# Maxima twelve steps ahead of the scores in place of fourteen, in a fused sequence kernel on one core

## The reference, cut to what matters

```
x = x + time_mixing(layernorm(x))
nodes = {-1: layernorm(x)}
for c in range(6):                       # per sequence
    q = ew[c,0] * (nodes[c-1] @ We + be) # k, v the same way, from earlier nodes
    qh, kh, vh = heads of q @ Wq, k @ Wk, v @ Wv      # 8 heads of 16
    attn = softmax(qh @ kh.T / 4)        # 1024 x 1024 for each head
    nodes[c] = act_w[c] * ((attn @ vh) @ Wo) + q
x = x + layernorm(nodes[5])
```

## Time and profile before

| what | us |
|---|---|
| median of three runs | 2273.95 |
| span of the profiled execution | 2273.4 |
| PE busy | 2241.8 (99%) |
| DVE busy | 2053.9 (90%) |
| ACT busy | 1830.3 (81%) |
| POOL busy | 527.6 (23%) |
| fill, from the first maxima matmul to the first score | 58.7 to 105.9 |
| last score, last matmul | 2251.7, 2264.0 |

### The profile page before, as it was taken

How to read it: one execution, slowest core, us unless ns; L and a number is a source line. 1 busy time by engine, 2 the same in 40 slices (tenths; PEclk the granted TensorE clock), 3 DMA queues, 4 the chain that set the end, 5 groups by cost and what they waited for, 6 DMA issues and landing times.

```text
span 2273.4 us, 46471 instructions
## 1 busy us (share of the span) xinstructions
PE 2241.8 (99%) x18091; PEld 855.8 (38%) x18091; DVE 2053.9 (90%) x2255; ACT 1830.3 (81%) x3431; POOL 527.6 (23%) x667
## 2 busy tenths in 40 slices
PE   7999999999999999999999999999999999999997
PEld 3534333333334333333333333333333333333332
DVE  6998999999999999999999998999999999999994
ACT  4267888888888888888888888888888888888885
POOL 4331330221312202202212112112023022321403
PEclk9999999999999999999999999999999999999999
DMA  4130322423313314224223223133133132342201
GB/s 129 59 67 23 81 65 55 84 67 67 79 46 91 71 33 91 60 61 91 57 57 82 61 61 79 39 86 79 31 73 77 36 82 59 71 84 53 58 26 51
DMA packets 86394, 149.17 MB, mean 66 GB/s; under 512 B 34250, under 2 KB 48926, under 8 KB 86174
## 3 DMA queue, kind: packets, MB, share of 16 engines
q0 software_dynamic: 28224, 94.13, 19.0%
q1 hardware_dynamic: 57950, 52.07, 9.0%
HBM read 41.97 MB, written 14.91 MB: 25 GB/s over the span
## 4 chain that ended last, share of the span: by engine, by line
PE 95%; DVE 2%; issue 1%; ACT 1%; SPq 0%; POOL 0%; DMA 0%; POOLq 0%; ACTq 0%; DVEq 0%
PE ring L536 44%; PE context L584 37%; PE ring L478 2%; PE ring L487 2%; PE ring L467 2%; PE ring L459 2%; PE ring L492 2%; PE wide L562 2%; DVE max_neg L1122 1%; PE context L413 1%; PE ring L356 1%; PE ring L381 0%; PE ring L378 0%; PE ring L392 0%; PE ring L382 0%
## 5 line engine op out<-in xcount | busy, mean ns | idle before, releaser
L1122 DVE TENSOR_REDUCE max_neg<-wide 128x1 f32<-128x1024 f32 x1536 | 1849.6, 1219 | 145.3 <-PE wide L562 139.1
L842 ACT ACTIVATE e_ring<-ring 128x512 f32<-128x512 f32 x3072 | 1667.8, 597 | 295.3 <-PE ring L536 153.6
L536 PE MATMUL ring<-q_aug,k_aug 50*128 50x512 f32 x3072 | 1126.2, 445 | 0.0
L562 PE MATMUL wide<-k_aug,q_aug 48*128 48x512 f32 x3072 | 1123.5, 445 | 1.9 <-DVE max_neg L1122 0.9
L584 PE MATMUL context<-e_ring,v_aug 128*32 128x256 f32 (+1 forms) x10752 | 942.2, 422 | 1.4 <-ACT raw L857 1.4
L536 PEld LDWEIGHTS ring<-q_aug,k_aug 50*128 50x128 f32 x3072 | 460.2, 185 | 754.5 <-ACT e_ring L842 551.6
L562 PEld LDWEIGHTS wide<-k_aug,q_aug 48*128 48x128 f32 x3072 | 459.2, 185 | 12.0 <-issue 6.5
L584 PEld LDWEIGHTS context<-e_ring,v_aug 128*32 128x32 f32 x10752 | 212.3, 108 | 481.0 <-issue 344.7
L331 POOL DMA_DIRECT2D src<-node_dram x40 | 22.8, 570 | 633.5 <-PE ring L478 633.5
L1224 POOL CAST q_part<-q_part 128x512 fp32r<-128x512 f32 x46 | 28.1, 611 | 477.0 <-ACT q_part L767 302.1
L301 POOL DMA_DIRECT2D q_aug<-q_part x138 | 71.8, 521 | 126.3 <-PE ring L536 126.3
(11 more groups left out here) (233 smaller groups left out, 867.4 us busy)
## 6 DMA issues: line engine op xcount, KB each, us to landing
q_aug<-q_part POOLq DMA_DIRECT2D x138, 256.0 KB, 4.5
k_aug<-k_part POOLq DMA_DIRECT2D x138, 256.0 KB, 6.9
src<-node_dram POOLq DMA_DIRECT2D x40, 512.0 KB, 7.1
ctxT<-raw SPq DMA_DIRECT2D x380, 32.0 KB, 2.0
rden_bc<-rden_dram SPq DMA_DIRECT2D x23, 512.0 KB
node_dram<-node_ring SPq DMA_DIRECT2D x16, 512.0 KB, 2.9
q_aug<-rows_dram SPq DMA_DIRECT2D x192, 8.0 KB
node_ring<-in_L_attn_x SPq DMA_DIRECT2D x4, 512.0 KB, 5.0
```

Source lines behind the costliest of these rows:

```text
L536: e.matmul(bk[:, :], k_aug[first:first + AUG, u % 2, h // 2, chunk * P:(chunk + 1) * P].bitcast(F32R), q_aug[first:first + AUG, u % 2, h / ...
L562: done = e.matmul(wide[w % 2][:, half_of(kh)], q_aug[first:first + SPLIT, u % 2, h // 2, q0:q0 + P].bitcast(F32R), k_aug[first:first + SPL ...
L842: e.activation(e_ring[:, n % E_SLOTS, :], bank[where["st", n]][:, :], ACT.Exp, scale=EXP_SCALE).then_inc(a_exp, 1)
L1122: e.tensor_reduce(max_neg[:, G % 2, row:row + 1], wide[w % 2][:, :], AX_X, ALU.max, negate=True).then_inc(v_mx, 1)
```

## The change

`LOOKAHEAD` goes from 14 to 12. The prologue's turns keep their places relative to the start. Stages that the table put into steps -14 and -13 go to -12, the new first one; folds 1 and 2 go from -13 and -12 to -12 and -11.

```
-LOOKAHEAD = 14
+LOOKAHEAD = 12
...
-        FOLDS_AT, BIASES_AT, VALUES0_AT, ONES_AT = (-13, -12, -10, -8, -7), 24, (-4, -3), 4
+        FOLDS_AT, BIASES_AT, VALUES0_AT, ONES_AT = (-12, -11, -10, -8, -7), 24, (-4, -3), 4
...
-            turns_then_steps((7, 7, 8, 17, 17, 17, 17, 17, 18, 21, 24, 24, 28, 29, 30, 30, 31, 31, 32), (-14, -13, -12, -12, -9)),
+            turns_then_steps((7, 7, 8, 17, 17, 17, 17, 17, 18, 21, 24, 24, 28, 29, 30, 30, 31, 31, 32), (-12, -12, -12, -12, -9)),
```

## The result

The changed kernel takes 2514.23 us in the median of four runs (2512.39 to 2517.69), against 2273.64 for the kernel before beside it: a ratio of 1.1046, 95% interval 1.1009 to 1.1083. That is 240.6 us. The forecast was 2424, with a range up to 2455. The sign was right; the time is 90 us above the forecast and 59 above its range.

The account below looks back on a forecast made before the run. PE, 95% of the chain, was taken as the bound. 2273.4 - 4 (fill) + 31 (splits) + 83 (late rows) + 40 (clock) = 2423.4, given as 2424 against the median of the runs; 8-in-10 range 2320 to 2455.

Parts of the forecast that it names:

- The sign: Whole kernel: the change makes it slower, chance 0.92; faster by more than 0.2% got 0.04.
- Part 1, the fill: Fill before the first score: two steps fewer save PE work, gain 0 to 5.2 us, 4 taken.
- Part 2, the split: Steps 5, 13, 21, 29: PE waits for DVE's moved splits, 0.62 or 0.25 us each, 31 us in all.
- Part 3, the rows of group 1: Step 8: rows loaded behind the 512 KB spread land late, 3.6 us per unit, 83 us in all.
- Rival B: Step 8: rows not held by the spread, landing in 4.5 us; 2326 us, chance 0.22 with its variants.
- Part 4, the clock: Behind the step 8 wait: low clock costs 2.0 us in 20 units, 40 us; bounds 0 and 3.2 per unit.
- Rival A: Behind the step 8 wait: the clock holds, so no low-clock cost; 2384 us, chance 0.28.
- The other three groups keep 3 us or more: Rows of the groups other than group 1: loaded two steps before the need, so no wait, 0 us.
- POOL issues in the same order: POOL's queue: its order of issue is unchanged by the shorter lead; no cost was put on it.

Follow-up runs that it names:

- the last run: Twelve steps, all K transfers behind the load of group 2's rows, products moved off the splits with K's second half at step 9, against the kernel before: 2309.77 us.

## Why the prediction was wrong

**Part 1, the fill.** Right: -3.7 at the first score, for -4. By the window the fill is 5.0 us shorter (42.16 for 47.20), but it also starts 1.3 later.

**Part 2, the split.** Right in place and nearly in size: 34.1 us for 31. By itself, at fourteen steps, 29. Step 5 is cheaper than I thought (11.5 for 14). Step 29 is dearer (10.6), and 4.8 of that are the two units in which POOL's affine lies beside the split; most of the others cost 0.24, as forecast. That collision was not in the prediction.

**Part 3, the rows of group 1.** Right: 87.2 us for 83, 3.8 per unit for 3.6. Rival B fell with it: the 8 KB load took 7.40 us in the unit shown, not the 4.5 of the earlier trace rows. With the load ahead of the spread the wait is 0, so the order is the cause. Whether the load stands behind the spread because both are on one queue, or because both need the same engines, is not shown: at step 16 large transfers of another queue did the same.
   The Trainium skill ("DMA: Bandwidth & Descriptors", Queues, rings and completion order) has both halves of this. That the engines take one queue's work in order agrees with the 8 KB behind the 512 KB. It also says that an engine takes turns between the queues it has work for, a packet at a time; step 16 shows how little that helps a small transfer on SP's queue against six large ones on POOL's, which took it from 2.05 to 8.9 us in the run with the load ahead of the spread.

**Part 4, the clock.** This is the step that failed, by size. "I take 2.0, in 20 units: 40": it was 4.0 in 22 units, 88.1, and more than the upper bound of 3.2 that I had set. The bound came from one stretch of 6.4 us in the earlier trace rows, behind PE work of one column. At a real wait the clock is low for 6.8, 10.2 or 13.7 us, 10.1 on the mean of the 22. Of these 222 us 20 fall into the waits, as I had allowed for, and each of the other 202 costs 0.44. Four matmuls in the wait took all of it away, so it is shown. One row was no bound; 48 of the 90 us missed are here.
   Rival A rested on the reading of the Trainium skill by which a short wait need not lower the clock. The same page ("TensorE: Matmul & The Clock Gate", HAM oscillation — how this bites in real kernels) tells of a kernel in which each wait for a transfer, between short bursts, starts the next burst at the low clock. That is what happened, in 22 of 23 units, behind waits of 2.0 to 4.9 us; the one unit without it waited 1.5. Here the work between two waits is dense and a whole unit long, which is not the page's case.

**What was missed: step 16.** "The other three groups keep 3 us or more: their load stands two steps before the need with no spread ahead" looked only at SP's own queue. I had written that POOL issues in the same order, which is true; but POOL's order against SP's rested on a wait, `wait_split(s + 1)` in step 9, that at twelve steps waits for nothing. It cost 27.5 us here, and 97 when the wait at step 8 was taken away (48.5 and 48.7). The run with K behind both small transfers shows the cause by its absence. Most of the last 7 us are the low clock behind step 29 of two units, where a third wait had lost its object.

Open: why one stretch of the low clock falls into the fill of some versions (thirteen steps, the K transfers split) and not of others that differ only far behind it.

## What to carry to other kernels

When a constant shifts the time at which work is due, go through the waits that were written in terms of it: a wait that finds nothing to wait for any more removes an order between two queues, or lets two engines meet, though no line of either has changed. Price a repeated PE wait with the clock behind it: here 3.8 us of wait had 4.0 more in its wake, and a few dummy matmuls within the wait removed that part. And undo a late transfer before adding up the rest, since one wait hides the next: with the first gone, the second grew from 27.5 to 97 us.

## What the hardware showed that I had not expected

- The granted clock was 1.2 GHz for 6.8, 10.2 or 13.7 us at waits of 2.0 to 4.9 us ahead of step 8. In 14 of 22 units the phase began up to 2.6 us before the wait ended, in the others up to 1.4 behind it, and PE was busy for the rest. The longest phases stood at waits of 3.8 to 4.9. The length of the wait alone does not decide: ahead of step 16 of the run with the load ahead of the spread, a wait of 1.6 us had 6.8 us of low clock behind it and one of 2.0 had none.
- A 16 KB store on SP's queue took 2.05 us to be seen as done in the kernel before, 5.5 with three 256 KB transfers of POOL ahead and 8.9 with six, on the mean; an 8 KB load behind six took 11.
- A 128x512 float32 matmul with float32 weights appears as two records and took 0.86 us.
- A small DVE instruction (0.17 us) took 0.6 to 1.9 us while POOL was in an elementwise instruction with two inputs, and ended with it (20 cases in the last run, two in the changed kernel).
